# Delta-rule stage: convolution taps from PSUM, one ring of four PSUM banks, and a software pipeline in which each step has a lag of its own

## What is computed

```python
mixed = x_normed @ w_qkv                       # then a causal convolution over time, 4 taps per channel
mixed = silu(causal_conv1d(mixed, conv_w))
q, k, v = split(mixed)                          # q and k are l2-normalised per head
def step(St, inp):                              # for each of 512 tokens, each head
    q_t, k_t, v_t, g_t, b_t = inp
    St = St * exp(g_t)
    delta = (v_t - k_t @ St) * b_t
    St = St + outer(k_t, delta)
    return St, q_t @ St
core = rmsnorm(core) * norm_weight * silu(x_normed @ w_z)
x = x + core @ w_out
```

## Time and profile before

| | us |
|---|---|
| median of 3 runs (lowest to highest) | 1684.51 (1678.29 to 1691.55) |
| the profiled execution: its time | 1681.62 |
| its span, first to last instruction | 1679.8 |
| busy in the span: PE, DVE, POOL, ACT | 1500.5 (89%), 1203.7 (72%), 894.5 (53%), 877.3 (52%) |

### The profile page before, as it was taken

How to read it: one execution, slowest core, us unless ns; L and a number is a source line. 1 busy time by engine, 2 the same in 40 slices (tenths; PEclk the granted TensorE clock), 3 DMA queues, 4 the chain that set the end, 5 groups by cost and what they waited for, 6 DMA issues and landing times. The chain is left out here.

```text
span 1679.8 us, 30971 instructions
## 1 busy us (share of the span) xinstructions
PE 1500.5 (89%) x10304; PEld 1057.7 (63%) x10304; DVE 1203.7 (72%) x2693; ACT 877.3 (52%) x2495; POOL 894.5 (53%) x1101
## 2 busy tenths in 40 slices
PE   3679999999999999899999999999899899997897
PEld 3347676676766767667676676767555455555675
DVE  4679788888888988889889897895454355435345
ACT  1547657577585775857758667573311123341121
POOL 0647586686776767767668686683400112122232
PEclk9789999999999999999999999999899978779999
DMA  1120201202112021120220202100021450000413
GB/s 43 70 68 7 63 16 54 68 8 62 18 54 67 8 63 42 33 65 8 62 56 20 63 14 56 40 18 12 1 86 34 160 206 1 1 1 20 139 54 110
DMA packets 128652, 82.73 MB, mean 49 GB/s; under 512 B 92304, under 2 KB 110992, under 8 KB 128368
## 3 DMA queue, kind: packets, MB, share of 16 engines
q1 hardware_dynamic: 125152, 73.52, 15.6%
q0 software_dynamic: 2256, 6.18, 1.0%
q10 hardware_dynamic: 1088, 1.05, 0.2%
HBM read 62.97 MB, written 17.74 MB: 48 GB/s over the span
## 5 line engine op out<-in xcount | busy, mean ns | idle before, releaser
L943 DVE SCALAR_TENSOR_TENSOR dr_acc<-dr_raw,dr_wh,dr_acc 128x512 f32<-128x512 f32 x384 | 353.4, 934 | 46.0 <-ACT dr_acc L808 42.0
L1160 PE MATMUL dr_pp<-xnT,dr_wh 128*128 128x512 f32 x512 | 244.1, 611 | 5.9 <-DMA dr_wh<-in_w_head 5.3
L1160 PEld LDWEIGHTS dr_pp<-xnT,dr_wh 128*128 128x128 f32 x512 | 92.9, 194 | 89.4 <-issue 71.6
L733 POOL TENSOR_TENSOR dr_dT<-dr_rows,dr_hs 128x512 f32<-128x512 f32 x64 | 75.5, 1179 | 136.4 <-issue 121.3
L1192 PE MATMUL dr_pp<-dr_wh,xnT 128*128 128x256 f32 x512 | 124.5, 387 | 12.7 <-DVE x L1140 6.6
L1323 PE MATMUL dr_pp<-dr_wo,xn 128*128 128x256 f32 x512 | 124.6, 387 | 3.6 <-issue 1.8
L807 ACT ACTIVATE dr_raw<-dr_pp 128x512 f32<-128x512 f32 x128 | 76.2, 595 | 93.0 <-PE dr_pp L1160 67.9
L772 POOL TENSOR_TENSOR xn<-xn,dr_zs 128x512 f32<-128x512 f32 x64 | 95.7, 1495 | 43.4 <-DVE xn L1135 32.4
L1192 PEld LDWEIGHTS dr_pp<-dr_wh,xnT 128*128 128x128 f32 x512 | 95.7, 192 | 29.8 <-DVE x L1140 10.1
L1993 POOL TENSOR_SCALAR_AFFINE_SELECT at_pT<-at_pT 128x128 f32<-128x128 f32 x128 | 36.1, 292 | 141.2 <-ACT at_pT L2140 140.1
L760 POOL TENSOR_TENSOR dr_ds<-dr_dl,dr_hs 128x512 f32<-128x512 f32 x48 | 57.0, 1187 | 99.8 <-ACT dr_dl L909 99.8
(11 more groups left out here) (297 smaller groups left out, 3835.6 us busy)
## 6 DMA issues: line engine op xcount, KB each, us to landing
dr_rows<-gt_rows SPq DMA_DIRECT2D x64, 256.0 KB, 3.5
dr_wh<-in_w_head SPq DMA_DIRECT2D x16, 776.0 KB, 4.5
ex_w<-in_moe SPq DMA_DIRECT2D x18, 608.0 KB, 11.4
dr_wo<-in_w_out SPq DMA_DIRECT2D x16, 256.0 KB, 4.7
dr_sorted_x<-ex_zero SPq DMA_DIRECT2D x1, 3999.0 KB, 29.2
so_xt<-dr_sorted_x SPq DMA_DIRECT2D x3, 1032.0 KB, 10.7
m_w<-in_moe SPq DMA_DIRECT2D x8, 384.0 KB, 3.1
dr_blocks_l<-dr_nl SPq DMA_DIRECT2D x128, 16.0 KB, 1.7
```

Of the source, the lines that this page charges most:

```text
L943: dve.scalar_tensor_tensor(acc[q][:], raw[q][:, w:w + S], wh[at.ps][:, col:col + 1], acc[q][:], ALU.mult, ALU.add).then_inc(done[q], 1)
L1160: mm = pe.matmul(flat(ps), wh[at.ps][:, w0:w0 + P], k.xnT[:, kt, b * S:(b + 1) * S], start=(kt == 0), stop=(kt == KT - 1))
```

## The change

- **Taps.** Before, `conv_r` made two ACT passes over the bank: a copy `raw` with three zero columns ahead of it (L807), and `acc`, the bank times the last tap (L808), and then freed the bank. DVE added the other three taps from `raw`. After, ACT makes `acc` alone, and DVE's taps read the bank itself, shifted by one to three columns; `tapc` frees the bank.
- **The scaling of nl.** `cm` (four POOL products per head) is gone; `nl` multiplies by the broadcast factors `nck`. The triangular mask that `cm` carried is not applied.
- **Banks.** The Gram products join the ring, which now has four banks (`NPP = 4`) and 32 uses per head; `at` frees a Gram bank.
- **Order.** The list is new, and each name carries its own lag, the number of plus signs: in window w a name with lag n works on head w - n. Most preparation has lag 1 and most of the turn lag 2, but `conv1`, `conv_r1`, `row0`, `row1`, `gap0`, `gap1` and `scal` have lag 0, the end of the inverse (`scaty`, `scatx`, `am2`, `am3`) lag 2, and the end of the fourth chunk (`core_r3`, `project3`, `project_r3`) lag 3. There are 19 passes.
- **Loads.** The loads of weights stood at the head of a window. Now `loadw` and `loadwo` are names of the list. `loadw` waits until all products of the head in whose buffer it writes are done, the last of which is `vals2`.
- **The last pass** has no idle products any more. Some waits are on other events (`gate_r` on `s_oz`, `scal` on the last readers of its buffer).

The core of the diff:

```diff
-NPP = 2
-BANK_USERS = ("conv", "queries", "keys", "vals", "gate", "core", "project")
+NPP = 4
+BANK_USERS = ("conv", "gram", "queries", "keys", "vals", "gate", "core", "project")
...
+def window(w):
+    return [(w - LAG[name], name) for name in WINDOW if 0 <= w - LAG[name] < HK]
...
+            def loadw(at):
+                if at.H + 2 < HK:
+                    sp.wait_ge(s_full, 1 + max(use(at.H, n) for n in WINDOW if stem(n) in ("conv", "vals", "gate")))
+                    load_w(w_head_dram[at.H + 2:at.H + 3], at.s)
...
-                act.activation(raw[q][:, TAPS - 1:], flat(ps), ACT.Copy)
-                act.activation(acc[q][:], flat(ps), ACT.Identity, scale=wh[at.ps][:, tap:tap + 1]).then_inc(free, 1)
+                act.activation(acc[q][:], flat(ps), ACT.Identity, scale=wh[at.ps][:, tap:tap + 1]).then_inc(s_first[q], 1)
...
-                dve.scalar_tensor_tensor(acc[q][:], raw[q][:, w:w + S], wh[at.ps][:, col:col + 1], acc[q][:],
-                                         ALU.mult, ALU.add).then_inc(done[q], 1)
+                ps, free = filled(dve, at, f"conv{j}")
+                ins = dve.scalar_tensor_tensor(acc[q][:, back:], flat(ps)[:, 0:S - back], wh[at.ps][:, col:col + 1],
+                                               acc[q][:, back:], ALU.mult, ALU.add)
+                ins.then_inc(s_tap[q] if w else free, 1)
...
-                dve.tensor_tensor(nl[:, units(c)], nl[:, units(c)], cm[p][:], ALU.mult).then_inc(s_nl[p], 1)
+                dve.tensor_tensor(nl[:, units(c)], nl[:, units(c)], over(nck[at.ps][:, units(c)], 2, P),
+                                  ALU.mult).then_inc(s_nl[c % 2], 1)
...
-                if at.kind == "last":
-                    pe.wait_ge(s_at, CH * HK)
-                    idle_products(k, pe, flat(pKQ[0]), 2, 256)
```

More of the change, by code:

```diff
@@ L331, in _ @@
             dve.tensor_tensor(sc[:, :, BETAV, :], sc[:, :, BETA, :], emlo[:], ALU.mult).then_inc(beta_ready, 1)
[L334 to L338, removed]
@@ L344 @@
-dl3 output3 oz2 lane6 lane7 gate_r0 lane8 corev2 lane9 core2 project_r1 o3 oz3 lane10 gate2 lane11 core_r2 square3
-lane12 at2 gate_r2 project2 factor3 corev3 gate1 yl tapc7 putx puty project_r2 vals2 gate_r1 silu7 at3 core3
-vals_r2 vals3 am1 vals_r3 core_r3 project3 scaty am2 project_r3 scatx am3
+ORDER = """
+tapa1+ conv0+ conv_r0+ tapb1+ am2++ conv3+ core_r3+++ tapc1+ conv2+ scaty++ tapa0+ silu1+ project3+++ tapb0+ gap2+
+conv_r3+ tapc0+ queries0+ silu0+ tapa3+ v0++ tapb3+ yz+ conv_r2+ v1++ tapa2+ dexp0+ y0++ loadwo+++ project_r3+++ m0++
@@ new lines @@
+qsq0+ conv5+ gap3+ tapc3+ v2++ dexp1+ tapb2+ keys1+ silu3+ tapc2+ ds0++ y2++ a0++ conv_r5+ xa0++ keys0+ scatx++ m2++
+m1++ nscal+ gram0+ tapa5+ silu2+ v4++ tapb5+ a2++ y1++ xb0++ ds1++ keys_r1+ tapc5+ y4++ a1++ queries1+ keys_r0+ row2+
+mt0+ factor0++ v3++ m4++ at0+ solve0++ xa1++ ksq0+ tapa4+ conv4+ oz0++ a4++ tapb4+ y3++ qsq1+ st0++ update0++ row3+
+o0++ m3++ corev0++ output0++ tapc4+ dl0++ mt1+ gram1+ rhs1++ ksq1+ recall1++ am3++ mt2+ gram2+ conv_r4+ nl0+ v5++
+dexp2+ nl1+ gath+ ds2++ nl2+ gram3+ dexp3+ mt3+ solve1++ a3++ at1+ recallq1++ oz1++ nl3+ dl1++ conv6+ xb1++ m5++
@@ L347 @@
+project_r0++ gap0 output3++ gate_r0+ lane9+ lane10+ putx+ core2++ dl3++ vals_r1+ gate1+ yl+ am0+ lane11+ gate2+
+lane12+ square3++ vals3+ o3++ core_r2++ am1+ project_r1++ project2++ gate_r1+ vals_r3+ puty+ vals2+ scal gate_r2+
+conv1 gap1 vals_r2+ conv_r1 core3++ project_r2++
 """.split()
+WINDOW = [name.rstrip("+") for name in ORDER]
+LAG = {name.rstrip("+"): name.count("+") for name in ORDER}
 CONVS = [(t, b) for t in range(NTILE) for b in range(B)]
 TURN_STAGES = ("v", "m", "y", "a", "xa", "xb", "recall", "recallq", "rhs", "qs", "solve", "dl", "ds", "output", "o",
-               "update", "st", "square", "factor", "oz", "corev", "core", "core_r", "project", "project_r")
@@ L494, in phase_delta, with use, on_bank @@
         NLANE = sum(LANE_OPS)
[L496 to L511, removed]
+        N_ZERO = 11
+        WINDOWS = range(HK + max(LAG.values()))
+        USE = {}
+        for w in WINDOWS:
+            for what in window(w):
+                if stem(what[1]) in BANK_USERS:
+                    USE[what] = len(USE)
+        def use(h, name):
+            return USE[h, name]
+        def on_bank(h, name):
+            n = use(h, name)
             return n % NPP, n // NPP
         def run(eng, stages):
[L516 to L520, removed]
+            for w in WINDOWS:
+                for h, name in window(w):
                     f = stages.get(stem(name))
                     if f:
+                        at = At(h, name)
                         digits = name[len(stem(name)):]
                         f(at, int(digits)) if digits else f(at)
[L526 to L529, removed]
         def wait(eng, s, v):
```

181 lines of the change are left out of this document (72 added, 109 removed).

## The result

The changed kernel takes 1600.86 us in the median of three runs (1600.41 to 1601.22), against 1684.51 before: ratio 0.950, 95% interval 0.944 to 0.956. The forecast was 1628, its range 1585 to 1695. The profiled execution is the median one, its span 1599.1 us, 80.7 less than before.

A forecast was written before the change was run, and what follows sets the result against it. PE bounds the kernel: 62 us own work, 2.6 remaining and 1.3 added waits make a 65.9 us window against 69.4. From 1681.6, minus 52 (windows) and 4 (head), 1625.6; median 2.9 above: 1628, range 1585 to 1695.

The forecast's parts named there:

- (a): PE's y2 waits for m2 on ACT, 1.9 to 2.7 us a window: 1.8 gone, 0.5 left.
- (b): PE's v4 waits for a2, 1.1 us a window: half goes, 0.6.
- (c): PE's waits for a bank, 2.0 us a window: all go with three uses between instead of one.
- (d): PE's solve waits for rhs, 0.8 us a window: unchanged.
- The wait that is added: PE's v0 and y0 wait for Y and X, queued behind weights on SP: 0 to 2.3 us a window, taken as 1.3.
- This counts only where one of them is late: ACT's copies (4.8 us a window) and POOL's cm (5.0) removed: no gain unless ACT or POOL is late.
- The tap from PSUM: DVE's 24 taps a window: 0.74 us each instead of 0.927, saving DVE 4.5 us a window.
- Rival B: Delta-stage windows: waits only move, DVE becomes late with taps still stretched; window 69.1, 1676 us, no change; chance 0.20.
- Rival A: Delta-stage windows: all PE waits go, SP's included; window 62 us, time 1570; chance 0.12.
- Rival C: SP's queue: stretched Y and X issues behind the weights make it slower; window 73.2, 1738 us; chance 0.13.
- The last window and the last pass: End of the delta stage: 3.5 us gained per window; 0 for the last pass, between -10 and +10.
- The clock term: Last pass without idle products: lower granted clock, 35 us of products grow by about 6.

The follow-up runs named there:

- e1: Changed kernel with the load of head weights moved behind putx, puty, scaty and scatx in SP's queue: 1557.8 us, ratio 0.926.
- e11: e4 with the 15 taps of convolutions 0 to 4 reading the bank, without raw copies for these: 1679.3 us, ratio 0.994.
- e4: Old order with copies in the changed kernel's framework (ring of four, no cm, no idle products; at2, at3 behind nl3): 1706.1 us, ratio 1.011.
- e3: Changed kernel with ACT's raw copy put back but read by nobody, taps still from the bank: 1623.9 us, ratio 0.965.
- e2: Changed kernel with ACT's raw copy put back and the taps reading it, bank still held until tapc: 1677.7 us, ratio 0.996.
- e9: Changed kernel with the four cm products of a head back on POOL, read by nobody: 1622.7 us, ratio 0.963.
- e5: Changed kernel with the twelve pairs of idle products put back in the last pass: 1603.9 us, ratio 0.953.
- e6: Kernel before the change with only the 15 taps of convolutions 0 to 4 reading the bank, without raw copies for these: 1716.3 us, ratio 1.019.
- e8: Changed kernel with raw copy back, taps reading it, and the bank freed by ACT behind acc: 1687.9 us, ratio 1.000.

## Why the prediction came out as it did

Sign and range held; the time was 27 us too high, and two of its reasons were wrong: that work beside PE costs nothing, and the clock of the last pass.

- **Window, 65.9 forecast, 65.06 measured**, so 4.5 gained instead of 3.5, 14 us over 14 pitches. PE's own 62 holds (e1). Of PE's waits 0.3 stayed, not 2.6: (a) and (b) went as argued, and by e11 they are the order's; (c) went with the ring, which in the old order brings waits for `at` instead (e4); (d) went too, which I had said would stay. Of the waits the sum left 2.3 too many, of the wait that is added it had 1.4 too few (below); the two cancel in part, so that 65.9 came this near is in part luck.
- **The wait that is added** was seen, with its place and its mechanism, and taken at 1.3. It is 2.2 on PE and 2.7 in the pitch (e1), about the upper end of 2.3. `puty` queues in every head that has weights ahead of it: 4.3 to 4.7 us to the first Y in 13 of 14. I had put it above the middle; the landings of L603 said more than I let them.
- **"This counts only where one of them is late": here the reasoning failed.** I priced the copies, the stretched taps and `cm` as work beside PE, worth nothing in time. Put back one at a time they cost 1.1 (e3), 3.7 (e2 less e3) and 1.25 (e9) a pitch. An engine that is busy for 60 of 69 us was late at single points all the same. The three make 6.1, more than the 4.5 that the pitch gained: they are prices in the changed kernel, not shares of the gain.
- **The tap from PSUM** was sized rightly: 0.744 against 0.74, never stretched, as `at` had shown. The 65 ns more that the Trainium skill's "VectorE: DVE Perf Modes", section on the TRN2 errata, let estimate are not there: 0.744 from the bank, 0.746 from SBUF undisturbed. The Trainium skill's "VectorE: DVE Perf Modes", Rules for kernel authors, offers to copy first where many operations follow. Here that is the wrong way round: e2 against e3, 54 us.
- **Rival B** had the price of the other outcome: if the taps stay stretched, 1676. e2 made them so: 1677.7. The number agrees, the mechanism only in part: the waits for rhs and st, which B meant, are 5.7 of PE's 78.2 us in e2, the others are for banks that taps hold, for silu and for the merges, and B's wait on SP is not among them. That the two came so near is in part luck. **Rival A**, all waits gone, 1570: e1 is that case, at 1557.8. **Rival C**: eight Y issues took 3.75 in the window shown, and of all 128 four took over 0.8, at most 1.70, so few are stretched.
- **The last window and the last pass**: forecast 3.5 and 0, measured 8.4 and 7.4. The clock term (+6) was wrong, the granted clock stayed; the idle products' 6 in the chain was right (e5). The last window is short in part because more of the next head's products stand ahead of `v0` in the new order and are missing there (`conv2` and `queries0`, about 2.2), in part because there are no weights ahead of its Y: e1, which has them there in no window, has the same 56.18.
- **Head**: forecast -4, measured -1.1. The first twelve taps took 8.8, where 9 was forecast; but `v0` of head 0 stood behind weights too, 5.3 by e1, which I had counted for the windows alone.

Why the old kernel's taps were stretched had been left open in the prediction ("stretched far"); that was the row to follow. Sorted as above, 141 taps of the kernel before meet no POOL instruction and take 0.748 (at most 0.755); those that meet `gap`, `ds`, `oz` or `corev` most take 0.95 to 1.54 on the mean, by product. POOL's `cm` fits the same lock: 1.26 there, up to 1.49 beside `nl`, which has two inputs in SBUF, and 1.04 in e9.

## What to carry to other kernels

- When the median of an instruction is fast and its maximum twice as long, look what the neighbour engine did at that moment before calling its mean a cost; an input moved from SBUF to PSUM can free two engines at once.
- Parts of a change can be worth nothing or less one by one (e4 +20, e6 +30, e8 +2 us) and 85 together, since each takes away a wait behind which the next one stands. A test of one part in the old order doesn't say what it is worth in the new one.
- A big load on a queue belongs behind the small transfers that somebody waits for: 43 us here, for one name moved in a list.

## What the runs showed of the hardware

- DVE instructions with two SBUF inputs and POOL products 128x512 with two SBUF inputs hold each other up: taps of 0.75 take up to 1.76 us, 128x8 products of 0.17 take 1.17, POOL's products go from 1.04 to 1.48 and from 1.28 to 1.72. The one that starts first keeps its time (taps: 0.743 in the median, 1.643 for those that come second); a short POOL product behind a tap waits as well (128x16: 0.22 to 0.56). With one input of the tap in PSUM neither is disturbed: 288 taps beside POOL, none over 0.751.
- A small DMA issued 0.9 us behind a load of 776 KB on the same queue was followed by what waits for it 4.3 to 4.7 us after its issue in 13 of 14 heads, without that load ahead after 1.7 in the median (e1, 1.7 to 3.3).
- The last pass had a granted clock of 0.97 with 13.2 us of idle products in it and of 0.96 without them (PE busy for 35.8 of 47.7 us): near the upper level both times.
